# Layer 2 feedforward, layer 3 attention and layer 3 cross attention of a four-layer decoder, joined into one pipeline over four sequences

## What is computed

```python
def _layernorm(x, axis=-1, eps=1e-05):
    ...
    return (x - m) / jnp.sqrt(v + eps)
...
# layer 2 feedforward: no experts, 128 -> 512 -> 128
h = layernorm(x, ln1_w, ln1_b)
h = bitlinear(h, w1, b1)
h = jax.nn.gelu(h, approximate=False)
h = layernorm(h, ln2_w, ln2_b)
out = bitlinear(h, w2, b2)
# bitlinear rounds x by row (127 / largest |x|) and w to -1, 0, 1
...
# layer 3 attention: 16 heads of 64
pattern = jnp.einsum('bhid,bhjd->bhij', k, q) * scale
prob = jax.nn.softmax(pattern, axis=-2)
out = jnp.einsum('bhis,bhid->bhsd', prob, v)
...
return concat @ Wo + bo
...
# layer 3 cross attention: over the 16 heads of one token, heads of 8
energy = jnp.einsum('nhld,ngld->nlhg', q, k)
attn = jax.nn.softmax(energy / jnp.sqrt(jnp.float32(dm)), axis=3)
out = jnp.einsum('nlhg,ngld->nhld', attn, v)
...
out = (out - mu) / jnp.sqrt(var + LN_EPS) * ln_g + ln_b
return out @ Wo.T + bo
...
x = x + _L2_ffn_ref(_layernorm(x, axis=-1), ...)
x = x + _L3_attn_ref(_layernorm(x, axis=-1), ...)
x = x + _L3_xattn_ref(_layernorm(x, axis=-1), ctx_1024, ctx_1024, ...)
```

## Time and profile before

| | us |
|---|---|
| median of 3 runs | 1222.85 (1214.53 to 1223.45) |
| the profiled execution, its own time | 1219.4 |
| its span | 1217.5 |
| feedforward, 657.4 to 736.6 | 79.2 |
| attention's layernorm and prelude, to 763.8 | 27.2 |
| attention, steps 0 to 20, to 794.2 | 30.4 |
| attention, steps 21 to 85, to 992.7 | 198.5 |
| its last output, to 1005.6 | 12.9 |
| cross attention, to 1091.0 | 85.4 |

### The profile page before, as it was taken

One profiled execution on the slowest core, in us unless ns is written; L12 is line 12 of the kernel. 1 busy time (PEld: TensorE's weight loads), 2 busy tenths in 40 slices (PEclk: granted clock), 3 DMA queues, 4 the chain that ended last, 5 costly groups with the idle time before them and its releaser, 6 DMA issues. The chain is left out here.

```text
span 1217.5 us, 15783 instructions
## 1 busy us (share of the span) xinstructions
PE 854.6 (70%) x5985; PEld 608.7 (50%) x5985; DVE 608.8 (50%) x1358; ACT 349.6 (29%) x672; POOL 291.0 (24%) x276
## 2 busy tenths in 40 slices
PE   5965887936661846888886117999999985029895
PEld 2542544824430834776543005667686773015794
DVE  3655834233899435756643893423232116964222
ACT  1110673311111120454553203243423221002231
POOL 2363102032287141322201001000000005744232
PEclk9975997966686876999988556989999998568998
DMA  9202101710000061435610000000000000003585
GB/s 385 81 3 89 53 4 36 205 45 18 0 1 0 1 133 33 101 84 139 170 31 1 0 1 1 1 1 2 1 2 2 1 1 0 0 0 129 178 280 169
DMA packets 44676, 72.42 MB, mean 59 GB/s; under 512 B 4817, under 2 KB 36737, under 8 KB 43033
## 3 DMA queue, kind: packets, MB, share of 16 engines
q1 hardware_dynamic: 38921, 65.72, 18.2%
q0 software_dynamic: 1728, 3.59, 0.8%
q10 hardware_dynamic: 3952, 2.10, 0.6%
HBM read 58.65 MB, written 15.89 MB: 61 GB/s over the span
## 5 line engine op out<-in xcount | busy, mean ns | idle before, releaser
L218 POOL TENSOR_SCALAR var_eps<-moments 128x8 f32<-128x8 f32 x8 | 1.9, 243 | 430.8 <-DVE moments L210 430.8
L1063 DVE TENSOR_REDUCE space<-PS 128x2 f32<-128x512 f32 x128 | 83.4, 686 | 40.3 <-PE PS L872 39.7
L617 DVE TENSOR_REDUCE space<-PS 128x2 f32<-128x512 f32 x64 | 43.6, 691 | 116.0 <-PE PS L2521 116.0
L2528 PE MATMUL PS<-space 64*128 64x256 f32 x256 | 81.2, 410 | 1.8 <-DMA space<-space 1.8
L1047 ACT ACTIVATE annex<-PS 128x384 f32<-128x384 f32 (+1 forms) x128 | 66.9, 545 | 51.6 <-PE PS L883 21.8
L560 PEld LDWEIGHTS PS<-space 128*128 128x128 f32 x512 | 62.1, 191 | 20.3 <-issue 20.3
L560 PE MATMUL PS<-space 128*128 128x65 f32 x512 | 70.8, 281 | 0.0
L2423 POOL TENSOR_TENSOR space<-space 128x1536 f32<-128x1536 f32 x16 | 54.6, 3438 | 39.3 <-ACT space L2296 33.0
L607 ACT ACTIVATE space<-PS 128x512 f32<-128x512 f32 x64 | 38.2, 597 | 81.2 <-PE PS L2529 81.2
L1354 PE MATMUL PS<-space 128*128 128x128 f32 x444 | 56.6, 282 | 6.1 <-issue 3.6
L1354 PEld LDWEIGHTS PS<-space 128*128 128x128 f32 x444 | 53.1, 196 | 8.1 <-issue 7.3
(11 more groups left out here) (487 smaller groups left out, 2268.1 us busy)
## 6 DMA issues: line engine op xcount, KB each, us to landing
space<-in_e_l_ffn SPq DMA_DIRECT2D x22, 768.0 KB
space<-in_e_l_ffn SPq DMA_DIRECT2D x23, 192.0 KB, 2.9
l_ffn_sorted<-in_slots SPq DMA_DIRECT2D x2, 1584.0 KB, 25.6
space<-l_attn_scratch_k SPq DMA_DIRECT2D x8, 384.0 KB
space<-l_ffn_sorted SPq DMA_DIRECT2D x10, 264.0 KB, 4.5
weights<-in_w_l_xattn SPq DMA_DIRECT2D x1, 2504.0 KB, 15.2
weights<-in_w_l_attn SPq DMA_DIRECT2D x1, 2124.0 KB, 11.7
space<-l_xattn_scratch_q SPq DMA_DIRECT2D x4, 512.0 KB, 3.4
```

The costliest lines, as they stand in the source:

```text
L617: nc.vector.tensor_reduce(MX[:, b % 2, :, h], PS[:, a % 3, :].rearrange("p (c k) -> p c k", c=2), AX_X, ALU.max).then_inc(max_done, 1)
L1063: nc.vector.tensor_reduce(m[:, :, at_h], PS[:, u % 3, :].rearrange("p (c k) -> p c k", c=2), AX_X, ALU.max).then_inc(max_done, 1)
L2528: nc.tensor.matmul(out, kk[:, 128 * kc:128 * kc + 128], q, start=True, stop=False)
```

## The change

`l2_ffn`, `l3_attn`, `l3_xattn`, `attention` and `attention_work` go, and `feedforward_attentions` stands in their place. It works by sequence, two tiles at a time, in one numbering of steps from -26 to 114. Steps 0 to 85 do what they did: the same 64 units, lag 21 (`WIDE_LAG`) and the order jobs, `first`, `second`, `weighted`. Two tables fill the rest. `place` puts a job of TensorE at the first step from the wanted one that has fewer than two; jobs alternate between banks 7 and 2, so `first` keeps two banks. `piece` puts a stretch of VectorE's, ScalarE's or GpSimd's work at a step. Sequence b's feedforward starts at `START[b]`, its cross attention right after its last output job, which is at steps 46, 62, 78 and 94. In cross attention all products are on GpSimd, and so are the subtraction of the maximum and the scaling by the denominator; maxima and denominators stand in SBUF. The quantisation finds the largest magnitude in one reduction of absolute values. The eight warm-up matmuls of `layernorm` (L225) are gone for these three blocks.

Jobs: w (sum of the weights' magnitudes), f1 and f3 (transposes), f2 and f4 (products) of the feedforward; T, the attention's input; q, k, v, M, t, o as before; xk, xv, xT, xq, xo, xw of the cross attention.

```diff
+def feedforward_attentions(c):
...
+    START = (-26, -15, 1, 16)
+    count, job_at, piece_at = collections.defaultdict(int), {}, collections.defaultdict(list)
+
+    def place(step, *job):
+        while count[step] >= 2:
+            step += 1
+        count[step] += 1
+        job_at[job] = step
...
+        place(16 * b + 18, "M", b, 0)
+        for i in range(6):
+            place(16 * b + 40 + i + i // 3, ("t", "t", "o")[i % 3], b, i)
+    first_x = [job_at["o", b, 5] + 1 for b in range(B)]
...
+        f = START[b]
+        for at, what in ((f, "in"), (f + 2, "twice"), (f + 4, "norm1"), (f + 5, "quant1")):
+            piece(at, what, b)
+        f = place(f + 7, "f1", b, 0)
+        f = place(f + 2, "f2", b, 0)
+        f = place(f, "f2", b, 1)
...
+        f = first_x[b]
+        piece(f, "cross", b)
+        place(f, "xk", b, 0)
+        place(f + 1, "xv", b, 0)
+        piece(f + 1, "normedx", b)
+        f = place(f + 2, "xT", b, 0)
+        f = place(f + 1, "xq", b, 0)
+        for i, what in ((1, "products"), (3, "sum0"), (5, "sum1"), (5, "shift"), (6, "expx"), (7, "dens"), (7, "values"),
+                        (9, "weigh0"), (12, "weigh1"), (12, "scale"), (13, "out"), (14, "normedo")):
+            piece(f + i, what, b)
+        f = place(f + 15, "xo", b, 0)
+        place(f + 1, "xw", b, 0)
...
+        def first(a):
+            b, h = a // HEADS, a % HEADS
+            if h % 4 == 0:
+                pe.wait_ge(*emptied("q", b, h // 4))
+                pe.wait_ge(*emptied("k", b, h // 4))
+            if a >= 2:
+                pe.wait_ge(max_done, a - 1)
...
+        for step in range(FROM, TO):
+            for job in [(i,) + j[1:] for i, j in enumerate(jobs) if j[0] == step]:
+                run_job(*job)
...
+            if 0 <= step < UNITS:
+                first(step)
+            i = step - WIDE_LAG
+            if 0 <= i < UNITS:
+                second(i)
+            if 1 <= i <= UNITS:
+                weighted(i - 1)
...
+            elif what in ("sum0", "sum1"):
+                t = int(what[3])
+                dve.wait_ge(multiplied, 4 * b + t + 1)
+                nc.vector.tensor_reduce(e[:, t, :], PR[:, t, :].rearrange("p (m d) -> p m d", d=8), AX_X, ALU.add).then_inc(summed, 1)
+                if t == 1:
+                    dve.wait_ge(summed, 2 * b + 2)
+                    nc.vector.tensor_reduce(mx[:, b % 2, :], e.rearrange("p t (h g) -> p (t h) g", g=16), AX_X, ALU.max).then_inc(maxed, 1)
...
+            if what == "products":
+                if b == 0:
+                    pool.wait_ge(*emptied("f4", B - 1, 0))
+                pool.wait_ge(*emptied("xq", b, 0))
+                pool.wait_ge(*emptied("xk", b, 0))
+                for t in range(2):
+                    if b >= 1:
+                        pool.wait_ge(summed2, 2 * (b - 1) + t + 1)
+                    nc.gpsimd.tensor_tensor(PR[:, t, :].rearrange("p (h g d) -> p h g d", h=16, g=16), bcast(heads(QX, t), 2, 16),
+                                            bcast(heads(KX, t), 1, 16), ALU.mult).then_inc(multiplied, 1)
+            elif what == "shift":
+                pool.wait_ge(maxed, b + 1)
+                m = e.rearrange("p t (h g) -> p (t h) g", g=16)
+                nc.gpsimd.tensor_tensor(m, m, bcast(mx[:, b % 2, :], 2, 16), ALU.subtract).then_inc(shifted, 1)
+            elif what == "values":
+                pool.wait_ge(exped, b + 1)
+                pool.wait_ge(*emptied("xv", b, 0))
+                for t in range(2):
+                    pool.wait_ge(summed, 2 * b + t + 1)
+                    nc.gpsimd.tensor_tensor(PR[:, t, :].rearrange("p (h d g) -> p h d g", h=16, d=8),
+                                            bcast(e[:, t, :].rearrange("p (h g) -> p h g", h=16), 2, 8),
+                                            bcast(heads(VX, t).rearrange("p g d -> p d g"), 1, 16), ALU.mult).then_inc(multiplied, 1)
+            else:
+                pool.wait_ge(summed2, 2 * b + 2)
+                pool.wait_ge(dens, b + 1)
+                o = O[:, b % 2].rearrange("p t (m d) -> p (t m) d", d=8)
+                nc.gpsimd.tensor_tensor(o, o, bcast(den[:, b % 2, :], 2, 8), ALU.mult).then_inc(scaled, 1)
...
+            if step == FROM + 3:
+                nc.gpsimd.memset(MTR, 0.0).then_inc(fills, 1)
+                nc.gpsimd.memset(bout, 0.0).then_inc(fills, 1)
+            for p in pieces(step, "products", "shift", "values", "scale"):
...
-                if b == "l2_xattn":
+                if b in ("l2_xattn", "l3_attn", "l3_xattn"):
...
+                if b == "l2_ffn":
+                    programs.append(feedforward_attentions(c))
...
-BUILDERS = dict(l0_ffn=l0_ffn, l1_attn=l1_attn, l1_xattn=l1_xattn, l2_ffn=l2_ffn, l3_attn=l3_attn,
-                l3_xattn=l3_xattn, l3_ffn=l3_ffn)
+BUILDERS = dict(l0_ffn=l0_ffn, l1_attn=l1_attn, l1_xattn=l1_xattn, l3_ffn=l3_ffn)
```

More of the change, by code:

```diff
@@ L1 @@
+import collections
 import math
@@ new lines, in feedforward_attentions @@
+    first_x = [job_at["o", b, 5] + 1 for b in range(B)]
+    place(START[0] + 3, "w", 0, 0)
+    piece(START[0] + 3, "weights", 0)
+    for b in range(B):
+        f = START[b]
[4 more added lines that the diff above has]
+        f = place(f, "f2", b, 1)
+        piece(f + 1, "gelu", b)
+        for i, what in ((3, "hidden"), (5, "norm2"), (6, "affine2"), (7, "quant2")):
+            piece(f + i, what, b)
+        f = place(f + 9, "f3", b, 0)
+        f = place(f + 2, "f4", b, 0)
+        piece(f + 1, "attn", b)
+        piece(f + 3, "normed", b)
+        f = place(f + 4, "T", b, 0)
```

1036 lines of the change are left out of this document (438 added, 598 removed).

## The result

Faster: 1172.15 us median of 4 runs (1170.07 to 1175.91), against 1223.15 of 4 runs of before (1214.53 to 1226.69) on the same chip. The ratio is 0.9587, with an interval of 0.9533 to 0.964. The forecast was 1165, with a range of 1143 to 1199. The profiled execution took 1175.91, with a span of 1174.1.

What follows compares the result with a forecast made beforehand. VectorE was taken to limit the ends of the joined blocks and TensorE the middle. 46.0 + 55 + 213 + 63 = 377 us against 433.6 gave a span of 1161 and a forecast of 1165, range 1143 to 1199.

Steps and rivals of the forecast that it cites:

- (a): Start of the joined block, up to the first `first`: forecast 46.0 us.
- the fill: GpSimd's 128x4096 fill in the start, taking 3.54 us and holding VectorE's scaling of the weights: counted at 2.2 us.
- (b): Steps 0 to 20, up to the first `second`: forecast 55 us, 30.4 before.
- 21 times 1.06: TensorE's work in steps 0 to 20: 21 `first` products at 1.06 us each, 22.3 us.
- 20 times 1.06: TensorE's work in steps 0 to 20: 20 projections at 1.06 us each, 21.2 us.
- The rival of turns: Steps 0 to 20: VectorE and TensorE wait for each other, 68 to 90 us there, 1178 to 1200 in all; 15%.
- The better rival: Everything overlaps better: 47 us for steps 0 to 20, 209 for steps 21 to 85, 1151 or 1143 in all; 15%.
- (c): Steps 21 to 85, the full pipeline to the last `weighted`: forecast 213 us, 198.5 before.
- (d): Tail after step 85, the last cross attention up to its last addition: forecast 63 us, 98.3 before.
- the rival of GpSimd blocking VectorE: Tail and steps: VectorE's reductions wait for GpSimd's products, 16 of 5 us adding 80, 1200 to 1245 in all; 4%.
- The clock rival: Steps 0 to 84: TensorE's waits drop its clock, 4.6 us each at about 25 places, up to 1280 in all; 6%.
- (e): The rest of the kernel behind the joined blocks, not touched by the change: taken as 126.5 us.

Runs made afterwards that it cites:

- bout_later: Changed kernel with the attention's output bias product four steps later, behind f2 of sequence 0 instead of ahead of it; profiled execution 1170.22 us.
- warm_steps: Changed kernel with 18 idle matmuls whose result nobody reads, six each at steps 5, 8 and 11; profiled execution 1171.77 us.
- lag_even: Changed kernel with lag 20 instead of 21, so first and second of a step want the same half of the rows; profiled execution 1228.93 us.
- keep_warm: Changed kernel with idle matmuls: 8 before T of sequence 0, 6 each at steps 5 and 11, 30 awaiting the last cross attention; profiled execution 1159.09 us.
- cross_first: Changed kernel with sequence 3's cross attention statistics and scaling ahead of sequence 2's last sum, its transpose and queries one step earlier; profiled execution 1179.78 us.
- last_split: Changed kernel with the last sequence's second-tile cross attention products on VectorE, beside GpSimd's for the first tile; profiled execution 1170.61 us.

## Why the prediction was right

**(a) was 3.8 us short.** The sum of what was counted held within 2 us: 49.8 less 2.6 for the bias and 1.4 to 3.3 for the fill is 43.9 to 45.8, and 43.8 was forecast without the fill. Not every term did: VectorE is busy 32.65, where its pieces and the fill were counted at 29.1. What was left out is one step. The step that made the output bias was costed at nothing, with no cover named: 3.57 us of TensorE at half clock between f1 and f2, worth 2.4 to 2.7 on the chain (bout_later). The fill was named and put at 2.2. It held one scaling for 3.7 in place of some 0.4, and without most of it (a) was 1.4 to 1.7 shorter: that term is right in place, and its size lies between 1.4 and 3.3, since the pieces cost something themselves. By the Trainium skill's rule (SBUF — State Buffer, Who interferes with whom) taken alone (a) would have been 47.3; the first scaling, at 3.69, did lose nearly the whole fill, so there the rule was the better guide.

**(b) was right in its sum, 54.8 for 55, and not in its terms: that was luck.** The same code took 51.6 to 54.8. The forecast was 46.1 of work, 4 of waits, 5 for the clock. warm_steps, at full clock, has 42.78 busy, of which 4.0 are idle matmuls: the work is 38.8. From 38.8 the kernel after gets to 46.87 by half clock (8.1) and to 54.8 by waits (7.9). So work was over by 7.3, and clock and waits together under by 7.0; the clock of 0.81 also lies under the 0.85 to 1 that was named as a sign.

The step that failed is 21 times 1.06 and 20 times 1.06. Where two `first` stand next to each other they overlap, in opposite halves of the rows, and show as one group of four (kernel after, timeline of PE):

```profile
709.80 0.71 PE L2133 MATMUL PS<-space 64*128 64x256 f32 x4 [0.98 <-issue]
...
710.88 1.99 PE L2085 MATMUL PS<-XT,weights 128*128 128x256 f32 x8
```

Both take 1.08, and there are four such pairs (709.80, 732.86, 741.40, 746.54): 4.2 less. Only 18 of the 20 projections run here; k and q of step 0 stand ahead of the first `first` and had been counted in (a): 2.1 less. The 18 take 0.96 each where two stand together (1.93 for two at 722.51 in warm_steps): 1.8 less. These three make 8.1, a little more than the 7.3. The check that gave 1.06 its credit, 29 x 1.06 = 30.7 against 30.4, was luck too: in the kernel before, the first five `first` took 3.57 in all (763.80 to 767.37), 0.71 each; busy time in those 30.4 us is 28.05, and waits of 0.56 (at 788.06) and 1.79 (at 794.20) made up for the difference.

The rival of turns is out: with VectorE busy 40.3 and TensorE 38.8 with work, 47.0 is far from the 68 to 90 of turns. But it is not TensorE alone that sets the pace: in warm_steps VectorE has no idle time over 0.33 from 710.38 to 734.75, and waits for TensorE only behind that, 1.66 and 1.71. The better rival's 47 is what the same tables give with the clock up.

**(c) came out 1.8 above 213, and most of the reason is shown.** The overlap of `first` and `second` holds (lag_even: 0.86 a step more without it), and a plain step takes 2.32 (`first` at 790.73 and 793.05), as in the earlier trace rows. Of the 214.8, 3.6 go to one fall of the clock, by keep_warm's 211.2 from one execution; other executions fell further, to 221.5. "Start-up and small waits 3.3" was that term, and it came to about 5.

**(d) came out 1.9 below 63.** The chain came in the order written, but its middle sooner: xT of sequence 3 stood 23.3 us behind the last `weighted`, where 25 at the earliest was named as a sign, and its queries were there at 27.0 for 28.4; that is 1.4 of the 1.9. On it lie products of 4.45 and 5.34 and sums of 2.29, with GpSimd waited for at each. VectorE's scalings and sums were not held up, because the tables keep scalings off the products: the rival of GpSimd blocking VectorE did not come. cross_first and last_split show that its mechanism exists, though for scalings and for products of two SBUF inputs, not for the reductions that the rival spoke of. VectorE's normalising product (L2412, one input in PSUM) is not held either: 424 to 426 ns in all 32, the one at 976.41 beside a GpSimd product among them.

**The clock rival** had the price about right and the number too high: 25 possible falls were priced at 4.6 each. Three stretches at half clock came, two in (b) and one in (c), and cost some 11 us over the best (b) and (c) measured (7.8 and 3.6), 3.8 each. The granted clock over (c) is 0.98, as before.

**(e)** was taken as 126.5 from one execution. The old kernel itself gave 126.5 and 132.1. 7.1 of the 13.1 us between the forecast span of 1161 and 1174.1 are this, 2.6 the start.

## What to carry to other kernels

When a block becomes one pipeline with its neighbours, look first for what used to hide in the long stage and now stands on a short chain: here a 3.6 us product that nobody needed yet. A step's cost measured where jobs separate two matmuls is not its cost where they stand together, and a sum that fits its stretch may hold a wait that makes up for an error. And place VectorE's scalings and two-input products apart from GpSimd's products, but its sums freely beside them: two engines' products taken in turn, each beside the other's sum, won 3.3 us of tail where the same work at once won nothing.
